# Moving the last six steps of a sort behind the weighing of the first image in a fused conv, sort and combine stage

## The reference, cut to what matters

```python
x = x + _L0_conv_ref(_ln_c(x), ...)          # involution
t = t + _L0_ffn_ref(_ln_t(t), ...)           # experts: y_tok = ybuf[idx, pos] * (prb * kept), nan_to_num
x = x + _L1_conv_ref(_ln_c(x), weight, bias) # relu(conv3x3 + bias)
t = t + _L1_ffn_ref(_ln_t(t), ...)           # needs segment_max / segment_sum over edges by dst
```

## Time and profile before

| what | value |
|---|---|
| median of 3 runs | 7993.13 us (7982.27 to 8010.47) |
| the profiled execution's own time | 7991.42 us |
| its span in the trace | 7989.7 us |
| busy share of the span | PE 89%, DVE 67%, POOL 63%, ACT 27% |

### The profile page before, as it was taken

How to read it: one execution, slowest core, us unless ns; L and a number is a source line. 1 busy time by engine, 2 the same in 40 slices (tenths; PEclk the granted TensorE clock), 3 DMA queues, 4 the chain that set the end, 5 groups by cost and what they waited for, 6 DMA issues and landing times. The chain is left out here.

```text
span 7989.7 us, 97304 instructions
## 1 busy us (share of the span) xinstructions
PE 7120.7 (89%) x34853; PEld 5221.1 (65%) x34853; DVE 5327.8 (67%) x7812; ACT 2136.4 (27%) x4196; POOL 5064.7 (63%) x4822
## 2 busy tenths in 40 slices
PE   8899895999599999399999999999999999999568
PEld 5677674666334444277777777777777777777467
DVE  6777664777755441277777777777767777777588
ACT  5666654444221221011111111111111111111110
POOL 2444344777546362677777777777777777777573
PEclk9999997999799999699999999999999999999889
DMA  6112111222213442811111111211111111111257
GB/s 180 59 58 88 57 55 59 86 59 59 92 58 92 78 70 45 70 45 42 42 42 43 41 43 44 50 42 42 42 42 42 42 42 42 42 42 43 82 198 270
DMA packets 467804, 533.45 MB, mean 67 GB/s; under 512 B 243904, under 2 KB 386686, under 8 KB 445826
## 3 DMA queue, kind: packets, MB, share of 16 engines
q1 hardware_dynamic: 298658, 327.93, 15.1%
q0 software_dynamic: 149632, 72.60, 7.1%
q10 hardware_dynamic: 19296, 130.03, 4.1%
HBM read 263.12 MB, written 278.84 MB: 68 GB/s over the span
## 5 line engine op out<-in xcount | busy, mean ns | idle before, releaser
L1882 POOL DMA_INDIRECT e_row<-rows_dram,e_idx x3328 | 3165.0, 951 | 1022.9 <-issue 1014.5
L1777 PE MATMUL e_found<-e_pieces,e_hot 128*128 128x512 f32 x12288 | 3043.4, 400 | 0.0
L1777 PEld LDWEIGHTS e_found<-e_pieces,e_hot 128*128 128x128 f32 x12288 | 2245.2, 188 | 498.5
L1914 DVE TENSOR_TENSOR e_hot<-e_spread,e_lows 128x1024 fp32r<-128x1024 f32 x770 | 935.3, 1215 | 300.8 <-PE e_spread L1763 294.3
L1939 DVE TENSOR_TENSOR e_prod<-e_found,e_pick 128x512 f32<-128x512 f32 x768 | 530.1, 690 | 799.3 <-PE e_found L1777 793.9
L1847 ACT ACTIVATE e_ex<-e_dx 128x512 f32<-128x512 f32 x64 | 38.5, 601 | 2929.7 <-DVEq L1975 2929.7
L1944 DVE TENSOR_REDUCE e_row<-e_prod 128x16 f32<-128x512 f32 x768 | 785.3, 1023 | 0.0
L811 POOL DMA_INDIRECT yb_dram<-b_y,b_home x320 | 547.2, 1710 | 207.4 <-issue 103.6
L1790 PE MATMUL e_bank<-e_h,e_w 128*128 128x512 f32 x1024 | 521.1, 634 | 173.0 <-ACT e_hid L1837 173.0
L312 POOL COPY a_xr<-a_xp 128x1573 f32<-128x1573 f32 x104 | 223.3, 2153 | 546.2 <-DVE a_xp L605 406.8
L1799 PEld LDWEIGHTS e_bank<-e_w,e_hid 128*128 128x128 f32 x4096 | 497.7, 195 | 100.9 <-issue 100.9
(11 more groups left out here) (393 smaller groups left out, 10118.4 us busy)
## 6 DMA issues: line engine op xcount, KB each, us to landing
ys_dram<-e_y ACTq DMA_DIRECT2D x64, 1024.0 KB, 3.9
f_ye<-ys_dram SPq DMA_DIRECT2D x64, 1024.0 KB, 5.6
e_row<-rows_dram,e_idx POOLq DMA_INDIRECT x3328
res_dram<-e_st ACTq DMA_DIRECT2D x64, 768.0 KB
xb_dram<-a_blanks SPq DMA_DIRECT2D x8, 2580.0 KB, 31.7
b_tok<-xb_dram SPq DMA_DIRECT2D x80, 258.0 KB, 2.7
a_xr<-in_x SPq DMA_DIRECT2D x8, 2048.0 KB, 9.7
a_xs<-in_x SPq DMA_DIRECT2D x8, 2048.0 KB, 8.4
```

Of the source, the lines that this page charges most:

```text
L1777: mm = nc.tensor.matmul(found[k % 2][:].rearrange("p s c -> p (s c)"), hot[:, k % 2, g], pieces[:, q, g].rearrange("p s c -> p (s c)"), st ...
L1882: nc.gpsimd.indirect_dma_start(row[:, s, u], None, rows, bass.IndirectOffsetOnAxis(ap=idx[:, s, u:u + 1], axis=0)).then_inc(gath[s], 16)
L1914: nc.vector.tensor_tensor(hot[:, k % 2], spread[:].unsqueeze(1).broadcast_to([P, HG, P]), lows[:].unsqueeze(2).broadcast_to([P, HG, P]), A ...
```

## The change

The six steps no longer stand ahead of the slots. Planning starts at slot `FIRST + BEHIND` = -6 with 12 us of sorting a slot, so three steps fall in slot -6 and three in slot -5, each time after the addition that DVE does there. `sort_end` becomes -4 (it was -9), and all that hangs on it moves five slots: the key passes to -4, the comparison to -3, the counting on DVE to -2 to 1 and on PE to -1 to 2, the ranks to 2 and 3.

```diff
-EARLY = 10
+BEHIND = 4
...
-        g, left = FIRST, SORT_US
+        g, left = FIRST + BEHIND, SORT_US
         for z in range(begun, COUNT):
             kind = NETWORK[z][0]
-            if z < begun + EARLY and kind != "turn" and not turn_slot:
-                slot_of[z] = FIRST - 1
-                continue
             if left <= 0:
                 g, left = g + 1, left + SORT_US
...
-            for z in range(begun, COUNT):
-                if slot_of[z] < FIRST:
-                    sort_step(z)
```

## The result

The changed kernel took 8015.86 us (median of 13 runs, 8007.81 to 8023.72), the kernel before 7994.82 us (13 runs, 7982.27 to 8010.47). The ratio is 1.0024 with a 95% interval of 1.0016 to 1.0032: 0.24% slower, 13 to 26 us. The forecast was 18 us slower and within 0.3%.

The account below looks back on a forecast made before the run. DVE was taken to bound the stage up to the first convolution, PE from the fourth on. 14.7 us late at the first plus 3.5 us over three slots gave 18.2 us, median 8011 us, range 7990 to 8032.

Parts of the forecast that it names:

- The sort covered a wait: Stage start: without the sort DVE waits for constants until 2143.4, so weighing starts 10.4 us earlier and not 27.
- The key store's landing is uncovered: Ahead of the comparison: DVE waits for the second key store, landing in 7.7 us, with about half a microsecond covering it.
- The second portion stands ahead of the first convolution: PE's slot 0: counting pairs that DVE makes behind a 6.65 us weighing come first; first convolution 14.7 us late.
- The next three slots: From first to fourth convolution: counting and totals add 0.4 + 2.0 + 1.1 = 3.5 us.
- The lower clock: Rival, around the first convolutions: PE's clock falls at every added wait; 26.6 us, slower by 0.33%; chance 0.18.
- Counting taken up by the convolutions: Rival, at the first convolutions: neither counting portion holds PE up; kernel 4.5 us faster; chance 0.10.
- The searches: POOL's searches start later, costed at nothing; cover of 7 us left before the third block.

Follow-up runs that it names:

- Constants first: Changed kernel with the five constants issued ahead of the loads of outputs and images; ratio to the kernel before 1.0016.
- sort ahead: Changed kernel with the six sort steps put back ahead of the weighing, all else left as changed; ratio to the kernel before 1.0007.
- Comparison later: Changed kernel with the comparison of neighbours and the small conversions ahead of it one slot later; ratio to the kernel before 1.0014.
- counting later: Changed kernel with the counting and the ranks three slots later on both engines; ratio to the kernel before 1.0006.
- before again: The kernel before, unchanged, profiled once more; stage 1159.2 us, rest of span 4717.6 us.

## Why the prediction was right, point by point

**The sort covered a wait.** Right, and to the microsecond: weighing at 17.9 us after the stage's start, 17.7 by the sum (2144.0 less 2126.3). Constants first and sort ahead show it from both sides: with the wait gone the stage follows, with the sort back the wait is gone. One step in it was wrong and did no harm: I had DVE at the wait after half a microsecond, but the cast and POOL's memsets kept it until about 2137.6, 9 us after the stage's start. That was still ahead of the constants; with constants first it is what is left.

**The key store's landing is uncovered.** Right in kind, mis-sized: 6.55 us from issue to the comparison where I took 7.7 from the earlier trace rows, inside the 1.5 us that I had allowed. Comparison later takes the wait away and the first convolution follows.

**The second portion stands ahead of the first convolution.** Right: PE's longest wait there is for it. The factors behind it took 2.22 us where I took 3.33 from the earlier trace rows. These two terms and smaller ones make the first convolution 12.7 us late and not 14.7.

**The next three slots.** 4.0 us against 3.5. The second convolution was 1.2 us slower than before (18.1 less 16.9), where I had 0.4: its factors took 2.86 us and not 1.88. The third came 2.0 us slower, as forecast, and the fourth 0.9 where I had 1.1.

The sum at the fourth convolution is 16.7 us (14.7 in the second profile of the changed kernel), 18.2 by forecast; the stage is 15.3 and 18.5 us longer in the two pairs, the time 19 us (0.0024 of 7994.82). That the time came within 1 us of the forecast is in part luck: two executions of one kernel differ by up to 2.4 us in the stage and by 16 us behind it.

**The lower clock.** This rival's price didn't come, but my argument against it didn't hold either. Busy time and granted clock (third from the end) in the changed kernel, in and behind the second portion, in and behind the third, and in the fourth:

```profile
2250.00:2252.00 2.00, 2.00 (x9) 0.52 (x8) 2.00 (x8) 0.00 (x0) 0.00 (x0) 0.50 0.04 8
...
2254.00:2256.00 2.00, 2.00 (x12) 1.23 (x11) 1.32 (x3) 0.00 (x0) 0.00 (x0) 1.00 0.00 0
...
2264.00:2266.00 2.00, 1.02 (x6) 0.35 (x6) 1.97 (x8) 0.66 (x1) 0.00 (x0) 1.00 0.00 0
...
2268.00:2270.00 2.00, 2.00 (x6) 1.01 (x7) 1.01 (x3) 0.00 (x0) 0.00 (x0) 0.50 0.00 0
...
2284.00:2286.00 2.00, 1.73 (x9) 0.74 (x8) 1.43 (x4) 0.00 (x0) 0.00 (x0) 1.00 0.00 0
```

The second portion ran at the lower level, 1.2 GHz, but the clock was back at 2.4 GHz ahead of the first convolution, so the 2 us that the rival added there did not come. The third portion began at 2.4 GHz, and the clock fell in it although DVE delivered a pair every 0.54 us: that PE isn't idle unbroken did not keep the clock up. The factors behind it took about 1 us more; the convolution after them ran at 7.89 us. In the fourth portion the clock stayed at 2.4 GHz. So the two portions behind the first convolution cost 1 us by the clock, and not 3.2 each. The Trainium skill, "TensorE: Matmul & The Clock Gate", section "HAM oscillation", would have each burst start throttled after a wait; the trace agrees for the second portion, behind a wait of 8.09 us, while the third and fourth began at 2.4 GHz behind waits of under 1 us.

**Counting taken up by the convolutions.** This rival had the front right and left out a term. In counting later neither portion holds up the first convolution, and that comes 4.6 us before the one of the kernel before, where the rival said 4.5; but PE then pays 8.5 us for counting in slots 2 to 6 and 4.3 us behind the rank chain. The Trainium skill, "Perfetto Trace Analysis", section "Optimization Strategy", holds that interleaving stretches with different busiest engines may help: against the changed kernel it did here, by 17.3 us at the first convolution, of which 11.1 are left at the tenth.

**The searches.** Costless, as forecast, but by 2.0 us and not 7: the two blocks took 90 us, from 2305.61 to 2395.66.

**Where leads shift.** The lead or lag of a kernel shifts by up to some 5 us between the tenth convolution and the last, also between the two executions of the kernel before (0.3 us apart at the tenth, 3.6 at the sixteenth). The traces show where. PE in order of time around the fifteenth convolution, in the kernel before and then in before again:

```profile
2430.78 3.04 PE L1238 MATMUL c_pm<-c_xs,c_cmat 128*128 128x512 f32 x4 [3.67 <-DVE c_xcb L1507]
2433.62 3.45 PE L1307 MATMUL c_misc<-c_wg,c_xcb 128*128 128x24 f32 x16
2436.89 10.38 PE L1318 MATMUL c_conv<-c_xp,c_w 128*128 128x512 f32 x18
...
2429.28 3.14 PE L1238 MATMUL c_pm<-c_xs,c_cmat 128*128 128x512 f32 x4 [3.67 <-DVE c_xcb L1507]
2432.22 2.39 PE L1307 MATMUL c_misc<-c_wg,c_xcb 128*128 128x24 f32 x16
2434.45 7.97 PE L1318 MATMUL c_conv<-c_xp,c_w 128*128 128x512 f32 x18
```

PE waits 3.67 us for DVE in both. Behind the wait the granted clock is still 0.50 in the first at 2439 to 2441, in the second 1.00 from 2433.5 on, and the convolution takes 10.38 us in the one and 7.97 in the other. Not settled: why the lower clock lasts longer in one execution than in another, and the 3 us by which executions differ between the last convolution and the end of the stage.

## What to carry to other kernels

Before a block of work is moved off the front of a stage, look up when the transfers land that the next instruction of its engine waits for: the block may be the cover, and only what it takes beyond them is gained. When work moves by slots, follow each engine's order inside the slot, since a small product of a late engine (here a counting portion) that the bound engine reads first holds up all behind it. Follow also what hangs on the work that moves: in counting later the rank chain cost more than two portions. Work that is cheap while an engine idles has its full price under a stretch that this engine is bound by.

## What the runs showed of the hardware

POOL's memsets in the changed kernel, the first and the last:

```profile
2128.64 7.35 POOL L1179 MEMSET c_xp<- 128x8712 f32 x1
...
2136.50 0.51 POOL L1179 MEMSET c_rstdt<- 128x512 f32 x1
```

A DVE cast of 128 x 512 from int32 to bf16, begun at 2128.72, took 8.57 us beside them and ended at 2137.29, behind the last; moved behind them it took 0.43 us, and in the kernel before 0.42. The profile counts the whole time as busy. The Trainium skill, "SBUF — State Buffer", section "SBUF: two separate sides", says that DVE in some modes and GpSimd hold a shared pair of ports for a whole instruction; the three durations agree with it, though no run shows whether this cast runs in such a mode. Here it cost nothing, because the set-up waited for the memsets or the constants anyway.
